# Other step numbers for the token-parallel operations of a recurrent layer

## The reference

```python
x1 = ln(layernorm(x));  xn = ln(x1);  dx = shift(xn) - xn          # shift: by one token
r, k, v = (xn+dx*x_r)@W_r, (xn+dx*x_k)@W_k, (xn+dx*x_v)@W_v        # and low-rank w, a, g
kk = k*k_k / norm_per_head(k*k_k);  k = k*(1+(a-1)*k_a)
# the scan, for t in 512 tokens, per sequence and head, state 8x8:
sa    = state @ (-kk_t)
state = state*decay_t + outer(sa, kk_t*a_t) + outer(v_t, k_t)
o_t   = state @ r_t
o  = groupnorm(o) + sum(r*k*r_k)*v;   x2 = x1 + (o*g) @ W_o
y  = x2 + relu(kf @ W_ffn1)**2 @ W_ffn2        # kf: ln(x2) mixed with its shift; 128 -> 512 -> 128
x  = x + y
h  = layernorm(x);  e = argmax(h @ W_router)                        # 4 experts
out = x + ln(gelu(h @ W1[e] + b1[e]) @ Wo + bo + h)
```

## Time and profile before

| | us |
|---|---|
| median of the runs | 1217.58 |
| the profiled execution | 1216.56 |
| its span, first to last instruction | 1214.7 |
| PE busy | 1043.4 (86%) |
| DVE busy | 890.9 (73%) |
| ACT busy | 668.6 (55%) |
| POOL busy | 629.7 (52%) |
| mean granted TensorE clock | 0.931 |
| chain that ended last: PE, DVE, ACT, "issue", DMA | 58%, 14%, 13%, 7%, 4% |

### The profile page before, as it was taken

How to read it: one execution, slowest core, us unless ns; L and a number is a source line. 1 busy time by engine, 2 the same in 40 slices (tenths; PEclk the granted TensorE clock), 3 DMA queues, 4 the chain that set the end, 5 groups by cost and what they waited for, 6 DMA issues and landing times.

```text
span 1214.7 us, 17920 instructions
## 1 busy us (share of the span) xinstructions
PE 1043.4 (86%) x5395; PEld 566.0 (47%) x5395; DVE 890.9 (73%) x2283; ACT 668.6 (55%) x1093; POOL 629.7 (52%) x885
## 2 busy tenths in 40 slices
PE   3666689989898989989898989999798989888866
PEld 2343354455454455455454555455454545454432
DVE  4567777887878787877878787887878787876220
ACT  2634464847475565747475665847475565734331
POOL 0346565565555565555555565555555565555100
PEclk8869899999898999989998999999998999989778
DMA  3101011111111121101111121111111121100110
GB/s 123 27 9 32 21 35 27 27 36 35 44 23 48 27 53 28 35 27 35 44 25 49 25 52 28 34 29 36 44 25 47 27 53 27 38 7 22 31 26 17
DMA packets 62759, 41.88 MB, mean 34 GB/s; under 512 B 7100, under 2 KB 56252, under 8 KB 62536
## 3 DMA queue, kind: packets, MB, share of 16 engines
q1 hardware_dynamic: 62664, 40.74, 13.7%
HBM read 11.35 MB, written 4.19 MB: 13 GB/s over the span
## 4 chain that ended last, share of the span: by engine, by line
PE 58%; DVE 14%; ACT 13%; issue 7%; DMA 4%; SPq 3%; ACTq 0%; DVEq 0%
PE fin_a L514 9%; PE fin_b L514 9%; PE sa_ps L359 9%; PE pre_a L298 6%; PE mid_ps L468 5%; PE fin_b L523 3%; DVE state L857 3%; SPq L262 3%; DMA rs_f<-row_ers 3%; PE mid_ps L298 3%; DVE upd L853 3%; PE vb_ps L338 3%; ACT hid L718 2%; DVE s_a L843 2%; ACT L548 2%
## 5 line engine op out<-in xcount | busy, mean ns | idle before, releaser
L1030 POOL TENSOR_TENSOR plus_kv<-state,kv 128x128 f32<-128x128 f32 x512 | 284.7, 556 | 418.5 <-DVE state L857 393.3
L359 PEld LDWEIGHTS sa_ps<-s_a,con 128*128 128x128 f32 x1024 | 183.6, 201 | 307.2 <-DVE s_a L843 230.3
L359 PE MATMUL sa_ps<-s_a,con 128*128 128x128 f32 x1024 | 237.5, 316 | 76.0 <-DVE s_a L843 75.9
L853 DVE TENSOR_TENSOR upd<-sa_ps,b_t 128x128 f32<-128x128 f32 x512 | 147.8, 289 | 169.5 <-PE sa_ps L359 164.8
L1022 POOL TENSOR_TENSOR s_r<-state,r_t 128x256 f32<-128x256 f32 x256 | 219.1, 856 | 1.3 <-DVE state L857 1.3
L857 DVE TENSOR_TENSOR state<-upd,plus_kv 128x128 f32<-128x128 f32 x512 | 175.2, 342 | 18.0
L843 DVE TENSOR_TENSOR s_a<-state,a_t 128x128 f32<-128x128 f32 x512 | 149.4, 292 | 18.5
L548 ACT ACT_TABLE_LOAD x101 | 129.6, 1283 | 1.8
L514 PE MATMUL fin_b<-h_e,mat 128*128 128x512 f32 x256 | 128.2, 616 | 0.8 <-ACT pick L733 0.8
L514 PE MATMUL fin_a<-h_e,mat 128*128 128x512 f32 x256 | 122.1, 593 | 0.0
L830 DVE TENSOR_TENSOR kv<-vb_ps,k_t 128x512 f32<-128x512 f32 x128 | 87.5, 684 | 0.3 <-issue 0.2
(11 more groups left out here) (197 smaller groups left out, 1733.9 us busy)
## 6 DMA issues: line engine op xcount, KB each, us to landing
rs_p<-row_rs SPq DMA_DIRECT2D x128, 64.0 KB, 2.1
x_in<-xT SPq DMA_DIRECT2D x16, 256.0 KB, 3.1
rs_p<-row_rk SPq DMA_DIRECT2D x64, 64.0 KB, 2.4
x_res<-xT SPq DMA_DIRECT2D x16, 256.0 KB, 2.9
rs_m<-row_frs SPq DMA_DIRECT2D x64, 64.0 KB, 2.1
rs_f<-row_ers SPq DMA_DIRECT2D x64, 64.0 KB, 2.1
rs_f<-row_lrs SPq DMA_DIRECT2D x64, 64.0 KB, 2.1
outT<-res SPq DMA_DIRECT2D x16, 256.0 KB, 2.3
```

The lines of the kernel that those rows point to most:

```text
L359: mm(sa_ps[:, 0:STATE], k("sum8"), s_a[:], start=True, stop=True).then_inc(s["sa"], 1)
L853: tt(ib(upd[:]), ib(sa_ps[:, 0:STATE]), over_i(b_t[c.slot][:, t * B:(t + 1) * B]), ALU.mult).then_inc(s["upd"], 1)
L1030: tt(plus_kv[:, (t % 2) * STATE:(t % 2 + 1) * STATE], st(t), kv[:, at:at + STATE], ALU.add).then_inc(s["plus_kv"], 1)
```

## The change

Only numbers in `AT` change. No instruction, tile, shape or wait is added or removed. The diff in full:

```diff
--- before.py
+++ after.py
@@ -25,20 +25,20 @@
 RING = 2
 
 AT = {
-    "c0": -32, "j0": -31, "sq0": -31, "rs0": -28, "x_in": -24, "xh0": -23, "x1": -22, "c1": -22, "sq1": -22,
-    "rs1": -22, "j1": -21, "xn": -19, "d_rs0": -18, "xh1": -17, "wa": -16, "dx": -16, "d_rs1": -15,
-    "mix_k": -15, "k": -15, "mix_g": -15, "th_w": -15, "mix_r": -15, "mix_v": -14, "w2": -14, "key": -14,
-    "th_d": -14, "rk": -14, "kks": -13, "val_tm": -11, "v": -11, "k2": -11, "cum": -10, "g1": -10,
-    "d_rk": -10, "p": -8, "val": -8, "k_t": -7, "kk": -7, "val_sb": -6, "r": -6, "kki": -5, "rkb": -5,
-    "rec": -4, "rkb_ps": -4, "r_t": -3, "b_t": -3, "a_t": -2, "g2": -2, "th_g": -1, "bonus": 0, "gate": 0,
-    "bonus_b": 23, "x_res": 34, "gj": 37, "gsq": 37, "grs": 38, "gxh": 39, "gaff": 39, "gg": 39, "wo": 41,
-    "x2": 42, "fsq": 42, "fc": 43, "x2x": 43, "frs": 44, "fj": 45, "xf": 46, "fxh": 48,
-    "hid": (50, 51, 53, 56), "kf": 51, "d_frs": 51, "f1": (52, 52, 53, 54), "f2": (55, 56, 57, 57),
-    "d_ers": 57, "y1": 58, "ec": 58, "ej": 58, "esq": 59, "h": 61, "router": 61, "ers": 62, "best": 62,
-    "onehot": 63, "masks": 63, "h_e": (65, 66, 69, 70), "pick": 66, "pick_sb": 66,
-    "moe": (68, 68, 70, 70, 70, 71, 71, 72, 73, 76, 76, 77, 78, 78, 79, 79), "act": (70, 71, 77, 77),
-    "y1b": 78, "mo": (80, 80, 81, 82), "lsq": 84, "y2": 85, "lrs": 85, "lj": 86, "d_lrs": 86, "store": 89,
-    "lxh": 91, "res": 91,
+    "c0": -32, "j0": -30, "sq0": -28, "x_in": -25, "rs0": -23, "xh0": -23, "d_rs0": -23, "d_rs1": -23,
+    "c1": -22, "x1": -21, "sq1": -21, "rs1": -21, "j1": -21, "xn": -18, "xh1": -17, "wa": -16, "dx": -16,
+    "mix_k": -15, "k": -15, "mix_g": -15, "th_w": -15, "mix_r": -15, "mix_v": -14, "w2": -14, "kks": -13,
+    "key": -12, "th_d": -12, "rk": -12, "v": -11, "k2": -11, "d_rk": -11, "val_tm": -10, "g1": -10, "cum": -9,
+    "p": -9, "val": -8, "val_sb": -8, "k_t": -7, "kk": -7, "r": -6, "kki": -6, "rkb": -5, "rec": -4,
+    "rkb_ps": -4, "r_t": -3, "b_t": -3, "a_t": -2, "g2": -2, "th_g": -2, "gate": -2, "bonus": 0,
+    "bonus_b": 26, "gj": 37, "x_res": 38, "gsq": 39, "gxh": 39, "gaff": 39, "gg": 39, "grs": 41, "wo": 41,
+    "x2": 42, "fsq": 43, "fc": 43, "x2x": 43, "frs": 45, "fj": 45, "xf": 48, "fxh": 48, "d_frs": 48, "kf": 51,
+    "hid": (52, 53, 54, 55), "f1": (52, 52, 53, 54), "f2": (55, 56, 56, 57), "d_ers": 58, "y1": 58, "ec": 58,
+    "ej": 58, "esq": 58, "h": 61, "router": 61, "ers": 61, "best": 63, "onehot": 63, "masks": 63,
+    "h_e": (65, 66, 69, 70), "pick": 66, "pick_sb": 68,
+    "moe": (68, 68, 70, 70, 70, 71, 71, 72, 73, 76, 76, 77, 78, 78, 79, 79), "y1b": 73,
+    "act": (74, 74, 77, 79), "mo": (79, 80, 81, 82), "lsq": 84, "y2": 85, "lrs": 86, "lj": 86, "d_lrs": 89,
+    "lxh": 90, "res": 90, "store": 93,
 }
 FIRST, LAST = -1, CHUNKS + 1
 DW = 64
```

## The result

The changed kernel takes 1225.1 us, the median of seven runs from 1221.57 to 1228.02; the kernel before took 1217.14 us beside it (seven runs, 1214.55 to 1219.43). The ratio is 1.0054, with a 95% interval of 1.0037 to 1.0070: slower by 4.5 to 8.5 us. The profiled execution took 1223.18 us, its span is 1221.4 us and the mean granted clock 0.937 (before: 1216.56, 1214.7 and 0.931).

The account below looks back on a forecast made before the run. PE's idle time in steps 26 to 3, paced by one chain, bounds the kernel. 0.32 + 0.2 = 0.5 us an iteration, 7 us over 14, nearly all taken back by the clock, leaves 1.5 us: 1219 us, range 1213 to 1229.

Parts of the forecast that it names:

- What bounds the kernel, and the mechanism: PE gapless from step 4 to mid step 26, moves there free; idle time in steps 26 to 3, paced by one chain.
- the chain to `h`: Steps 26 on: y1, ec, esq, ej, ers, the row's copy to all channels, then h, which the transfer ends.
- f2.2: Product moved ahead of SA(25): SA(26) then waits for s_a, making ec and h 0.32 us later.
- Step 26: kki, lxh, res moved there: kki hidden, step 27 lighter, s_a of step 28 at 649.9 instead of 649.40; h covers it.
- the late bound: s_a of step 28 at 650.6 us (estimate 649.9), with DVE and POOL blocking each other and bonus_b in step 26.
- best: Moved to step 31: onehot ends 0.3 us later, masks, SA(0) and c0 follow; cost 0.2 us (bounds -0.1 and 0.5).
- The 14 iterations that hold all four chunks: Iterations to which the 0.5 us applies: 7 us if each simply gets longer.
- Before the scan and behind it ... nothing: Outside the full iterations, orders are the same for the chunks that are left, so no cost.
- That takes back nearly all: Iterations fall in step with clock changes, 68.26 us mean; fewer long ones leave 14 x 0 to 0.2 us, forecast 1.5 us.
- the nothing for the other orders: mo.0, ACT moves, val_sb, cum, y1b, j0: taken as nothing; together they can be worth -0.1 to 0.3 us.
- the rival in which the sum is paid: Rival 1: the 0.5 us an iteration is paid in full, 1225 us, 1229 with late bounds; chance 0.42.

Follow-up runs that it names:

- e1_f2: Kernel before with only f2.2 moved ahead of SA(25): 1218.9 us, ratio 1.0005.
- e12_middle: Kernel before with only mo.0, act.2, lsq, cum, y1b and val_sb (ahead of the replications) in their new order: 1220.82 us, ratio 1.0018.
- e8_after_val_back: Changed kernel with val_sb alone back behind the two replications: 1223.75 us, ratio 1.0041.
- e9_before_fill: Kernel before with five filler matmuls an iteration in TensorE's idle time of steps 26 to 1: 1209.37 us, ratio 0.9918.
- e4_three_back: Changed kernel with f2.2, the step 26 group (kki, lxh, res, bonus_b) and best back at their old steps: 1221.99 us, ratio 1.0024.
- e5_delay2: Kernel before with two extra VectorE instructions in step 2 of each iteration, ahead of upd: 1224.53 us, ratio 1.0050.
- e7_after_f2_back: Changed kernel with f2.2 alone back behind SA(25): 1222.35 us, ratio 1.0037.
- The five parts alone: Kernel before with one part each: f2.2, step 26 group, best, orders of steps 0 to 11, remaining orders; ratios 1.0005, 1.0007, 1.0003, 0.9997, 1.0018.

## Why the prediction was right or wrong

**What bounds the kernel, and the mechanism: right.** The idle time of PE is in steps 26 to 3, the chain to `h` sets the pace there, and the moves in steps 4 to 25 are free: steps 14 and 15, 16 to 19, and 22 and 23 trade 0.3 to 0.7 us among each other in the profile after, with a sum of zero.

**f2.2: right in mechanism, the size a little low.** SA(26) waits for `s_a` as worked out and comes 0.34 us later. `ec` and `h` come 0.44 us later (12.95 to 13.39 us behind `s_a` of step 24), where I had 0.32: I had left out that an SA that is waited for takes 0.49 us and a queued one 0.38.

**Step 26: right.** `kki` is hidden (from SA(26) to `ec` it is 1.62 us with it and without it, in e1_f2), step 27 gives up 2.2 us and step 26 takes 2.1, `state` is still stretched (0.79 us), and what DVE gains ends in the wait for `h`. `s_a` of step 28 comes 10.36 us behind that of step 24 instead of 10.03, 0.3 us later, where I had 0.5 and at the latest 1.2. That DVE and POOL shut each other out showed at three places: `kki` 0.94, `res` 1.06, `bonus_b` 1.19 us where it had 0.69. By the Trainium skill ("SBUF — State Buffer", "Who interferes with whom") this was to be expected, and the trace agrees for these instructions; but the late bound that it spoke for was not reached, and `h` would have covered a part of it.

**best: wrong.** I had it at 0.2 us more an iteration. The delay of `masks` against `s_a` of step 30 is 0.1 us, not 0.3, as `score` took 0.17 us where it had 0.29; and steps 30 and 31 together are 0.3 us shorter where the clock falls in them (4.26 against 4.56 us) and of the same length where it does not (4.27 against 4.25, with filler). Alone its price is between -1.3 and 2.1 us in all. So the sum for a full iteration is not 0.5 us but 0.3, which the two kernels with filler show, and in a short iteration of the changed kernel, with the clock as it is, only 0.1 to 0.2 (67.64 against 67.49 us: 0.4 in steps 24 to 29, -0.3 in steps 30 and 31).

**"The 14 iterations that hold all four chunks": there are thirteen,** 2 to 14. That changes 7 us to 6.5.

**"Before the scan and behind it ... nothing": wrong.** The group of e12_middle costs 0.9 to 3.5 us, and not in the full iterations. I had compared the orders of the operations that are left before the scan, found `val_sb` and the replications exchanged, and costed that by the cover of a full iteration, which is not there before it. That the price of the group comes from this one order is argued and not shown: before the scan it accounts for a few tenths in most profiles and for 1.3 us in one, iteration 0 may add 1 us, and e8_after_val_back points the same way within its interval.

**"That takes back nearly all": no rule to cost by.** This step and the nothing for the other orders are where the forecast of 1219 us went wrong. The observation behind it is real. Without the slow stretches the two lengths vanish, and 10 us with them (e9_before_fill). With f2.2 alone 0.4 us an iteration disappeared in the mix of the two lengths, and in the changed kernel twelve of thirteen full iterations have the mean of before. But the slow stretches themselves change. The thirteenth took 70.76 us, and the profiles of e4_three_back, e5_delay2, e7_after_f2_back and e8_after_val_back have such iterations too, of 69.4 to 71.6 us. Two extra instructions in step 2 were paid in full by the medians; five cost 2.4 times their size. The whole change in the full iterations, 4.1 us with hardly any clock in it, came to 2.8 in the one profile, while the difference between the two kernels' medians is about the same with the clock's falls (8.0 us) as with the filler (7.5 us).

**The range** was right because it held the rival in which the sum is paid. That its 1225 us met the median exactly is luck: it came from an iteration sum that was too large (0.5 for 0.3 us) and from nothing for orders that cost about 2 us.

**What stays open.** The five parts alone add up to 0.30% with a margin of about 0.3, the whole is 0.54% (0.37 to 0.70); whether parts cost more together than alone is not decided by these runs. Nor is where the 2 us of e12_middle lie, why some slow stretches last until step 3 or 4, nor why a delay in step 25 is taken back and one in step 2 isn't.

## What to carry to other kernels

Where engines work through fixed lists, find the chain that ends each idle stretch, and cost a move by what it does to that chain: the moves elsewhere were worth nothing, although they shifted single steps by 0.3 to 2 us. Cost every exchange twice, once under the cover of the full loop and once in the fill and the drain, where the cover may be missing. When two single profiles differ by a few microseconds, look at the length of every iteration, and at the same stretch in a kernel that costs nothing, before you put the difference down to the change. And if TensorE's clock falls once an iteration, try filling its idle time first: five matmuls that nobody reads were worth more here than any order that was tried.

## What the hardware showed

The granted clock fell to 1.2 GHz once in nearly every iteration, behind steps 27 to 29, in which PE was busy for 5.28 of 8.40 us (645.15 to 653.55, before), its longest pause being 1.29 us; in steps 2 to 24 of the same iteration it was busy for 45.93 of 47.00 us (594 to 641), and the clock stayed at 2.4 GHz. Five filler matmuls in the idle time kept it at 2.4 GHz in 12 of 13 iterations and took 0.8% off the time. The other way round, a delay of 1.0 us in step 2 was followed by a second fall a few us later and cost 2.4 us.

VectorE and GpSimd held each other up: `bonus_b` took 1.19 us instead of 0.69 beside `lxh` and `res`, and `res` 1.06 instead of 0.75 beside `bonus_b`. The timeline shows this as longer instructions and not as idle time before them.
